# Graph attention by scattered rows on one core: half of x and eight tiles of sums read ahead of the last scatters

## The reference, cut to what matters

```python
h = maximum(layernorm(x), 0.0)                       # x: 8192 x 128
proj = einsum('nf,hfo->hno', h, W)                   # 4 heads, 128 -> 128
scores = leaky_relu(s_src[:, :, None] + s_tgt[:, None, :], 0.2)
attn = softmax(adj[None] + scores, axis=1)           # adj: 8192 x 8192, entries up to 1e9
vals = einsum('hij,hjo->hio', attn, proj) + h[None]
out = x + elu(vals).mean(axis=0)
```

## Time and profile before

| | |
|---|---|
| median of 3 runs | 882.7 us (881.6 to 883.72) |
| the profiled execution | 881.85 us, span 880.0 us |
| DVE, ACT, PE busy | 788.3, 673.4, 695.0 us |
| ACT exponentials of chunks | 512, 559.3 us |
| scatters | 64, median 7.3 us to landing |
| adj | 268 MB in 184 transfers |

### The profile page before, as it was taken

One profiled execution on the slowest core, in us unless ns is written; L12 is line 12 of the kernel. 1 busy time (PEld: TensorE's weight loads), 2 busy tenths in 40 slices (PEclk: granted clock), 3 DMA queues, 4 the chain that ended last, 5 costly groups with the idle time before them and its releaser, 6 DMA issues.

```text
span 880.0 us, 15010 instructions
## 1 busy us (share of the span) xinstructions
PE 695.0 (79%) x5016; PEld 586.6 (67%) x5016; DVE 788.3 (90%) x836; ACT 673.4 (77%) x1183; POOL 261.9 (30%) x163
## 2 busy tenths in 40 slices
PE   0292488897897898797978978978978888898994
PEld 0281478786786687686877877866967777884441
DVE  3797899899999999999999999999999897975997
ACT  0083397797797887977967977879789679897995
POOL 1000013214233332412331333223123221344996
PEclk9997699899899999999999999999899899999998
DMA  9999999999999999999999999999999999926913
GB/s 326 350 346 392 373 373 368 374 364 371 368 372 371 372 370 368 375 370 372 371 368 372 372 371 372 370 368 375 370 372 371 368 364 295 290 55 165 280 53 86
DMA packets 224012, 294.44 MB, mean 335 GB/s; under 512 B 4707, under 2 KB 218212, under 8 KB 223974
## 3 DMA queue, kind: packets, MB, share of 16 engines
q1 hardware_dynamic: 214226, 289.49, 95.8%
q0 software_dynamic: 9216, 4.20, 4.0%
q10 hardware_dynamic: 532, 0.27, 0.1%
HBM read 281.29 MB, written 12.65 MB: 334 GB/s over the span
## 4 chain that ended last, share of the span: by engine, by line
DMA 29%; DVE 28%; PE 20%; issue 13%; SPq 7%; ACT 3%; DVEq 0%; ACTq 0%; POOLq 0%
DMA arena<-in_adj 23%; PE ps L572 12%; DVE arena L768 11%; SPq L441 7%; DVE arena L793 6%; PE ps L538 5%; DMA sums<-arena 4%; DVE ps L798 3%; DVE arena L785 2%; ACT ps L683 2%; PE ps L621 2%; DVE arena L761 1%; DMA checked<-arena 1%; DVE arena L993 1%; DVE arena L959 1%
## 5 line engine op out<-in xcount | busy, mean ns | idle before, releaser
L683 ACT ACTIVATE ps<-ps,arena 128x1024 f32<-128x1024 f32 x512 | 559.3, 1121 | 159.2 <-PE ps L572 111.0
L572 PE MATMUL ps<-ident,arena 128*128 128x128 f32 x4096 | 538.0, 283 | 20.8 <-ACT ps L683 19.6
L572 PEld LDWEIGHTS ps<-ident,arena 128*128 128x128 f32 x4096 | 469.2, 146 | 76.1 <-ACT ps L683 71.7
L768 DVE TENSOR_TENSOR arena<-arena 128x3072 f32<-128x3072 f32 (+1 forms) x120 | 360.1, 3001 | 13.7 <-DMA arena<-in_adj 9.3
L502 POOL DMA_INDIRECT sums<-arena x64 | 161.1, 2517 | 529.1 <-DVE arena L835 288.8
L538 PE MATMUL ps<-ident,arena 128*128 128x128 f32 x512 | 81.1, 310 | 144.1 <-DVE arena L785 132.4
L538 PEld LDWEIGHTS ps<-ident,arena 128*128 128x128 f32 x512 | 66.5, 161 | 155.3 <-DVE arena L785 79.1
L683 ACT ACTIVATION_READ_ACCUMULATOR ps<-ps,arena 128x1 f32 x512 | 123.0, 240 | 0.0
L793 DVE TENSOR_REDUCE arena<-ps 128x1 f32<-128x1024 f32 x64 | 78.2, 1222 | 21.9 <-PE ps L538 21.4
L785 DVE TENSOR_TENSOR arena<-arena 128x1024 f32<-128x1024 f32 x64 | 76.5, 1221 | 7.4 <-DMA arena<-in_adj 6.8
L798 DVE SCALAR_TENSOR_TENSOR ps<-ps,arena 128x1024 f32<-128x1024 f32 x64 | 82.1, 1282 | 0.0
(11 more groups left out here) (89 smaller groups left out, 241.4 us busy)
## 6 DMA issues: line engine op xcount, KB each, us to landing
arena<-in_adj SPq DMA_DIRECT2D x160, 1536.0 KB, 14.9
arena<-in_adj SPq DMA_DIRECT2D x8, 1024.0 KB, 10.3
arena<-in_adj SPq DMA_DIRECT2D x16, 512.0 KB, 7.4
sums<-arena SPq DMA_DIRECT2D x1, 4160.0 KB, 23.7
out<-arena SPq DMA_DIRECT2D x15, 256.0 KB, 2.7
arena<-sums SPq DMA_DIRECT2D x6, 512.0 KB, 7.9
sums<-arena POOLq DMA_INDIRECT x64, 7.3
arena<-sums SPq DMA_DIRECT2D x4, 256.0 KB, 3.1
```

The costliest lines, as they stand in the source:

```text
L572: mm = pe.transpose(turned_ps[buffer_of(g, i, n)][:, m, :], piece(g, i, r)[:, m, q * P:(q + 1) * P], ident[:, :])
L683: act.activation(turned, turned, ACT.Exp, scale=KAPPA, bias=cert[:, i, q, G:G + 1], accum_out=cert[:, i, q, r:r + 1]).then_inc(f_exp, 1)
L768: dve.tensor_tensor(acc_of(g, i), acc_of(g, i), piece(g, i, r), ALU.max).then_inc(f_acc, 1)
```

## The change

In the order of the diff:
- **SP**: the two early reads now wait for the first chunk of the last strip and for all but the last two scatters. Behind them go two quarters of x, and only then the waits for the last chunk and the last scatter.
- **POOL**: the scatter of set 62, not that of set 63, waits for the early reads.
- **PE**: behind the last strip's sixth exponential come `sums_ahead` (the part of set 62 for both groups, by marks of its own) and both `add_sums`, all ahead of the opening of the banks and of the last strip's `turn_idx`. `last_sums(0)` and `(1)` add set 63 to it, the first ahead of `sum_same`.
- **DVE**: `mark_ahead` marks set 62's targets in the last strip, ahead of `find_target` of strip 22. Strips 20 and 21 get one common running maximum, 128 x 2048 a piece (`twin_max`), in strip 19, with `find_target` of strip 18 still behind the fifth; the later strips' maxima all move up (in strips 21 and 22 likewise). A narrow strip's `find_rows` is two instructions instead of four. `stage_sums(0)` goes ahead of the last `find_target`, `stage_sums(1)` ahead of `check_rows`.
- **PE's order**: in strip 19 the maxima of its second and third set are turned one chunk later (`late`), those of strip 20 too (`NEXT_AT` 21).
- **ACT**: twelve tiles of h are normalised at the end of the first strip, and from then on nine tiles ahead; the places of `turn_idx`, `sum_same` and `copy_sum` in the last five strips change (`INDEX_AT`).

```diff
+    def both_acc():
+        return acc[:, 0:2 * RT * P].rearrange("p (k t j) -> p k t j", k=2, t=RT)
+    def pieces_ahead(Q):
+        if isinstance(Q, int) and Q > STRIPS - NARROW:
+            return (Q - 1) * (G - 2)
+        return Q * (G - 2)
...
     def index_at(g, i):
-        if known(g) and number(g, i) in SOON:
-            return SOON[number(g, i)]
+        if known(g) and number(g, i) in INDEX_AT:
+            return INDEX_AT[number(g, i)]
...
-    LAST_NORM_AT = 4
-    SOON = {STRIPS - NARROW - 1: (8, 10, 11)}
-    NEXT_AT = {STRIPS - NARROW - 1: 20, STRIPS - NARROW: 6, STRIPS - NARROW + 1: 6, STRIPS - NARROW + 2: 6}
+    NORMS = 3 * NQ
+    INDEX_AT = {STRIPS - NARROW - 1: (8, 13, 13), STRIPS - NARROW: (3, 4, 4), STRIPS - NARROW + 1: (3, 4, 3),
+                STRIPS - NARROW + 2: (3, 5, 4), STRIPS - 1: (2, 3, 3)}
+    NEXT_AT = {STRIPS - NARROW - 1: 21, STRIPS - NARROW: 6, STRIPS - NARROW + 1: 6, STRIPS - NARROW + 2: 6}
...
+    X_AHEAD = 2
...
-            sp.wait_ge(f_turn, NT * G)
-            sp.wait_ge(f_added, (NT - 1) * 16)
+            sp.wait_ge(f_turn, (NT - 1) * G + 1)
+            sp.wait_ge(f_added, (NT - 2) * 16)
+            def load_rows(j):
+                sp.dma_start(x_rows[j], x_t[:, j * XT:(j + 1) * XT, :]).then_inc(t_x[j], 16)
...
                 if k == EARLY:
+                    for j in range(X_AHEAD):
+                        load_rows(j)
+                    sp.wait_ge(f_turn, NT * G)
...
-                if t1 % XT == 0:
-                    j = t1 // XT - 1
-                    sp.dma_start(x_rows[j], x_t[:, j * XT:(j + 1) * XT, :]).then_inc(t_x[j], 16)
+                if t1 % XT == 0 and t1 // XT > X_AHEAD:
+                    load_rows(t1 // XT - 1)
...
-                    if last_strip(g, i):
+                    if known(g) and Q == STRIPS - 2:
...
+                late = 1 if known(g) and Q == STRIPS - NARROW - 1 else 0
...
-                    if nq == NQ and n % LEAD == LEAD - 1 and n // LEAD + 1 < nq:
-                        turn_maxima(g, i, n // LEAD + 1)
+                    if nq == NQ and n - late in (LEAD - 1, 2 * LEAD - 1):
+                        turn_maxima(g, i, (n - late) // LEAD + 1)
...
+            def add_sums(k):
+                pe.wait_ge(t_agg[k], 16)
+                for u in range(QUAD):
+                    pe.matmul(agg_ps[k % 2][:, u * P:(u + 1) * P], agg[:, k * QUAD + u, :], ident[:, :], start=False, stop=True,
+                              skip_group_check=True)
+            def sums_ahead(k):
+                pe.wait_ge(t_ahead, k + 1)
+                pe.wait_ge(f_h, NT - 1)
+                pe.matmul(agg_ps[k % 2], h[:, NT - 2, 0:F], hot_ahead[:, k * QUAD * P:(k + 1) * QUAD * P], start=True, stop=True)
...
-                pe.matmul(agg_ps[k % 2], h[:, NT - 1, 0:F], hot[:, k * QUAD * P:(k + 1) * QUAD * P], start=True, stop=True)
-            def add_sums(k):
-                pe.wait_ge(t_agg[k], 16)
-                for u in range(QUAD):
-                    mm = pe.matmul(agg_ps[k % 2][:, u * P:(u + 1) * P], agg[:, k * QUAD + u, :], ident[:, :], start=False,
-                                   stop=True, skip_group_check=True)
-                mm.then_inc(t_turn, 1)
+                pe.matmul(agg_ps[k % 2], h[:, NT - 1, 0:F], hot[:, k * QUAD * P:(k + 1) * QUAD * P], start=False, stop=True,
+                          skip_group_check=True).then_inc(t_turn, 1)
...
+            pe.wait_ge(f_exp, NT * G + BUFFERS - 2)
+            for k in range(EARLY):
+                sums_ahead(k)
+            for k in range(EARLY):
+                add_sums(k)
...
+            last_sums(0)
...
-            last_sums(0)
-            add_sums(0)
+            last_sums(1)
...
-            last_sums(1)
...
-            add_sums(1)
...
                     if not first_strip(g, i) and n == NORM_AT:
-                        layer_norm(*former_of(g, i))
-                    if last_strip(g, i) and n == LAST_NORM_AT:
-                        layer_norm(g, i)
+                        layer_norm(sets_to(g, i) + NORMS, NQ)
...
-            def layer_norm(g, i):
-                for q in range(subs(g, i)):
-                    t = sets_to(g, i) + q
+                    layer_norm(0, NQ + NORMS)
+            def layer_norm(first_tile, tiles):
+                for q in range(tiles):
+                    t = first_tile + q
+                    if isinstance(t, int) and t >= NT:
+                        return
...
-                    dve.wait_ge(f_acc, Q * (G - 2) + r - 1)
+                    dve.wait_ge(f_acc, pieces_ahead(Q) + r - 1)
...
+            def twin_max(r):
+                Q = STRIPS - NARROW
+                new = both(r).rearrange("p t (k j) -> p k t j", k=2)
+                if r == 1:
+                    wait_landed(dve, *TWIN, 0)
+                    wait_landed(dve, *TWIN, 1)
+                    old = both(0).rearrange("p t (k j) -> p k t j", k=2)
+                else:
+                    wait_landed(dve, *TWIN, r)
+                    dve.wait_ge(f_acc, pieces_ahead(Q) + r - 1)
+                    old = both_acc()
+                dve.tensor_tensor(both_acc(), old, new, ALU.max).then_inc(f_acc, 1)
...
-                    dve.wait_ge(f_acc, (Q + 1) * (G - 2))
+                    dve.wait_ge(f_acc, pieces_ahead(Q) + G - 2)
...
+                if nq == 1:
+                    dve.scalar_tensor_tensor(junk[:, 0, :], cert[:, i, 0, 0:G], 0.5, range_at, ALU.is_ge, ALU.mult,
+                                             accum_out=base[:, 0:1]).then_inc(f_base, 1)
+                    dve.wait_ge(f_base, Q + 1)
+                    dve.wait_ge(f_up, sets_to(g, i) + 1)
+                    dve.tensor_scalar(idx[:, i, 0:1], base[:, 0:1], in_range[:, i, 0:1], N - 1.0, ALU.add, ALU.min).then_inc(f_idx, 1)
+                    return
...
+            def ahead_of_twin(g, i):
+                before = former_of(g, i)
+                last_max(g, i, 0)
+                last_max(g, i, 1)
+                column_max(g, i, 0)
+                last_max(g, i, 2)
+                column_max(g, i, 1)
+                find_rows(*before)
+                column_max(g, i, 2)
+                twin_max(1)
+                twin_max(2)
+                find_same(*before)
+                twin_max(3)
+                twin_max(4)
+                twin_max(5)
+                find_target(*before)
+                twin_max(6)
+                last_max(*TWIN, 0)
...
                 if k == 0:
-                    piece_max(*after, 1)
-                    piece_max(*after, 2)
-                    last_max(g, i, 0)
-                    for r in (3, 4, 5, 6):
-                        piece_max(*after, r)
+                    last_max(*after, 0)
+                    piece_max(*next_but_one, 1)
+                    column_max(g, i, 0)
+                    piece_max(*next_but_one, 2)
+                    find_rows(*before)
+                    piece_max(*next_but_one, 3)
+                    find_same(*before)
+                    piece_max(*next_but_one, 4)
+                    piece_max(*next_but_one, 5)
+                    find_target(*before)
+                    piece_max(*next_but_one, 6)
...
+                    dve.wait_ge(t_at, 1)
+                    dve.wait_ge(f_idx, STRIPS - 1)
+                    for k in range(EARLY):
+                        mark_ahead(k)
...
+                    return
+                if known(g) and number(g, i) == STRIPS - NARROW - 1:
+                    ahead_of_twin(g, i)
...
+            def mark_ahead(k):
+                cols = slice(k * QUAD * P, (k + 1) * QUAD * P)
+                dve.tensor_scalar(hot_ahead[:, cols], row_at[:, cols], idx[:, (STRIPS - 2) % BODY, 0:1], None,
+                                  ALU.is_equal).then_inc(t_ahead, 1)
...
-            dve.wait_ge(t_at, 1)
...
+            stage_sums(0)
...
-            stage_sums(0)
+            stage_sums(1)
...
-            stage_sums(1)
```

More of the change, by code:

```diff
@@ L191, in peaked_path @@
     hot = ring[:, 3, 2 * RT * P:2 * RT * P + EARLY_TILES * P]
+    hot_ahead = ring[:, 1, 2 * RT * P:2 * RT * P + EARLY_TILES * P]
     assert EARLY_TILES * P <= RT * P
@@ L247, in peaked_path @@
     t_hot = sem("last_targets_marked")
+    t_ahead = sem("targets_ahead_of_last_marked")
     t_turn = sem("tail_sums_turned")
@@ L878, in narrow_strip @@
                 if k == 0:
-                    piece_max(*after, 1)
-                    piece_max(*after, 2)
-                    last_max(g, i, 0)
-                    for r in (3, 4, 5, 6):
-                        piece_max(*after, r)
+                    last_max(*after, 0)
[9 more added lines that the diff above has]
+                    piece_max(*next_but_one, 6)
+                elif k == 1:
                     column_max(g, i, 0)
@@ L886, in narrow_strip @@
                     last_max(*after, 0)
+                    piece_max(*next_but_one, 1)
                     find_same(*before)
-                    for r in (1, 2, 3, 4):
```

(23 more changed lines are left out.)

## The result

The changed kernel takes 887.82 us (887.25 to 889.41, 4 runs), the kernel before, measured beside it, 882.77 us (4 runs): ratio 1.0056, 95% interval 1.0037 to 1.0074. It is slower by 5.1 and 6.5 us; I had forecast 3.5 us (886.2 us, range 880.6 to 889.0). Its profiled execution took 887.66 us, 5.8 more than that of before.

The account below looks back on a forecast made before the run. The end bounds the kernel: a relay of scatters, then ACT's chunks. Relay 4.4 us late, early reads and x beside set 62's scatter make the last read 3.5 us late: 885.35 us profiled, 886.2 against 882.7; range 880.6 to 889.

Parts of the forecast that it names:

- The body and the start: Body instructions unchanged; nine more norm tiles at the first strip's end, where ACT idles 28.25 us, cost nothing.
- The join into strip 20: Strips 19 and 20: third set 1.6 us later, then 13.1 us to strip 18's targets; relay of scatters 4.4 us late.
- The issue beside a wide maximum: First scatter of the relay, issued while DVE runs a 2,048-wide maximum: 1.1 us more, between 0 and 2.4.
- Set 59 and ACT's stand: Strip 22: set 59 lands at 784.0 instead of 779.85; ACT stands 4.4 us before copying strip 21's sums.
- Set 62's scatter: Behind the early reads, beside 6.3 us of x: takes 6.0 us, bounds 3.3 and 6.8, landing at 801.9.
- PE's path: Marked products and adds before the last rows: turned at 799.0 instead of 796.18, last target near 801.5 instead of 798.35.
- The read: Read of the next four tiles behind the last scatter: there at 808.7 instead of 805.2, 3.5 us late.
- the last one, from the read to the third pair: End of the kernel: the read's 3.5 us delay added whole to the profiled time, 881.85 + 3.5 = 885.35 us.
- Half of x ahead hides nothing: Tail: x ahead gains nothing, since nothing waited for x; counted inside the forecast, with no chance of its own.
- The faster case: ACT's relief in strip 22 reaches the end: last exponential 3.1 us earlier, 879.6 us; chance 0.17.
- The "no change" rival: Relay makes good its 4.4 us, set 59 lands at 780: 0.5 us less, 882.2 us; chance 0.20.

Follow-up runs that it names:

- the repetition: The changed kernel unchanged, measured again later beside the other experiments: 888.63 us, ratio 1.0067 to the kernel before.
- a_target3: The changed kernel with strip 18's targets written behind the third wide maximum instead of the fifth: 884.49 us, ratio 1.0024 to the kernel before.
- a_x0: The changed kernel with all of x read behind the last scatter again, none ahead: 886.57 us, ratio 1.0057 to the kernel before.
- a_busy: The changed kernel with five more products on PE behind the second pair's projection, in its wait: 886.04 us, ratio 1.0047 to the kernel before.
- c_x2: The same as c_x0, but with half of x read ahead, as in the change: 884.22 us, ratio 1.0021 to the kernel before.
- b_new_tail: The kernel before with only the changed end; strips, norms and places as before: 886.0 us, ratio 1.0047 to the kernel before.
- a_pairs: The changed kernel with pairs 3 and 4 projected ahead of the turning of tiles 8 to 11: 883.82 us, ratio 1.0016 to the kernel before.
- c_before: The kernel before with only pairs 3 and 4 projected early, staging and turning in mended places: 884.04 us, ratio 1.0023.
- c_x0: The changed kernel without x ahead, strip 18's targets behind the third wide maximum, pairs 3 and 4 early in mended places: 880.73 us, ratio 0.9970.

## Why the prediction was right, and where its terms were off

**The body and the start.** As forecast nothing came of the twelve norms ahead: 718.67 us for the last strip's maxima against 717.75, 0.9 late, less than executions of one order of strips differ by (717.38 to 718.67).

**The join into strip 20.** I took 1.6 us; the third set's reduction began 0.6 later (728.99 against 728.36). PE had its full clock there, where before's showed 0.66 in 720 to 725 us. In the repetition it was 0.50, and the reduction began at 730.83: 1.6 was inside the scatter. From that set's end to the targets I had 13.1 us and it was 12.5; the wide maxima took 2.29 to 2.31 each. The relay began at 744.90, not 746.4: 2.9 late, not 4.4. That this costs was right, and a_target3 shows it.

**The issue beside a wide maximum.** 2.91 us against 1.57, 1.3 more; I had 1.1, and 1.5 by the Trainium skill's rule on the port (SBUF — State Buffer, "SBUF: two separate sides"), which this fits.

**Set 59 and ACT's stand.** Forecast 784.0 and 4.4 us; measured 781.05 and 3.43. But in the repetition it was 784.15, in a_x0 783.9, for one and the same order of strips: with the late ones go a hole in the stream of adj at 725 to 730 us (241 and 242 GB/s, against 293 in the changed kernel's profile) and a lower clock of PE in 720 to 725 us (0.50 and 0.68, against 1.00). Which leads isn't shown. The value I named was inside the scatter of executions.

**Set 62's scatter.** This term of the sum was too small, and outside its bounds: 7.27 us, 7.46 in the repetition, where I took 6.0 from 3.3 to 6.8. The upper bound was the slowest of four scatters beside adj. The Trainium skill's rule (DMA: Bandwidth & Descriptors, "Queues, rings and completion order") would have had it near 3.3: here the rows disagree with what I drew from it, in all six kernels that read x there (7.03 to 7.46 us).

**PE's path.** Forecast: last rows turned at 799.0, last target at 801.5, close under the scatters. Measured 797.22 and 799.5, as the last exponential was earlier. It was hidden, by 2.5 us; without x it is the end (a_x0).

**The read.** 808.7 forecast, 808.93 measured. The path was right, and that its time was right to 0.2 us was luck. Set 59 landed 3.0 us sooner than forecast, and four terms took it back: set 62's scatter, 1.3 over; set 60, which landed 5.0 us behind set 59 and not 4.0, as ACT's copy and DVE's targets stand between them; the reads, there 3.7 us behind set 61 and not 3.1; and 0.4 in small gaps.

**What the sum lacked.** The step that failed is the last one, from the read to the third pair: I took the read's 3.5 us for the whole loss, and so carried before's 2.45 us over without a reason. PE stood 5.68 us where it had stood 0.43, the clock fell to half, and it took 4.6. This is nearly all of what is missing between 3.5 and the 5.8 us of the profiled executions, and a_busy shows it. Behind that pair ACT's pace had no gap, as forecast.

**The rivals.** "Half of x ahead hides nothing" was right, and half said: it costs 3.5 us where it lies on the path, with the clock's fall in it (c_x2). The faster case needed set 59 by 779.6 and a scatter of set 62 under 4 us; a_target3 gave the first, and without the second it was still 2.4 us over before. The "no change" rival has ACT end at 792.1 with set 59 at 780; by its own terms it is 792.4, which moves nothing.

## What to carry to other kernels

A transfer issued early to fill a gap runs beside the small dependent one that the end waits for, and here doubled its time (7.0 to 7.5 us for 3.3): ask which link of a serial chain is in flight while it runs, and count the chain with it. Before a wait is made longer on PE, look at which work behind it needs only what is already there, and at what PE's clock will be when it goes on. And take each part of a change out by itself, from a version where nothing else covers it: x ahead could not be told from nothing while PE's path lay close behind (a_x0), and cost 3.5 us in c_x2. A change of order can also cost where it wasn't aimed at, as the checks 30 us behind the moved pairs did.

## What was not expected of the hardware

- A scatter of 128 rows of 512 B took 7.03 to 7.46 us beside a read of 2 MB in 512 B rows (seven executions of six kernels), and 3.2 to 3.4 beside little else; beside adj it took 6.1 to 6.8 in most cases and 5.6 to 7.7 at the extremes, the first of each relay left out.
- PE's clock was granted at half after it had stood for 5.68 us (the changed kernel), 4.73 (its repetition) and 6.63 (a_target3), and fell to 0.72 of full in a window of 3 us after 3.77 (b_new_tail). It stayed at full after 3.14 (a_x0) and 2.02 (a_pairs), and with five products in the gap (a_busy). But in c_x2 it was at half after waits of 2.89 and 0.78 us, and in c_before after 1.71 and 0.49, where the kernel before kept it at full through 1.48 and 0.49: the length of one wait doesn't decide it. At half, the projections of two pairs took 5.4 us instead of 3.6 to 4.0.
- One order of strips gave set 59 anywhere from 781.05 to 784.15 us in six profiled executions.
- Three DVE instructions on 128x1 took 1.22 us each in c_x0, c_x2 and c_before, and 0.69 in four other traces.
